# One attention kernel, one edit: the product with V in one piece at the end of each block, and a new order of the work in a block

## The reference, cut to what matters

```
q, k, v = (qkv[0], qkv[1], qkv[2])             # 16 heads of width 16, 4096 tokens
scores = jnp.einsum('bhqd,bhkd->bhqk', q, k) / math.sqrt(hd)
scores = jnp.where(causal[None, None], -jnp.inf, scores)
attn = jax.nn.softmax(scores, axis=-1)
attn_out = jnp.einsum('bhqk,bhkd->bhqd', attn, v)
```

## Time and profile before

| | us |
|---|---|
| median of 3 runs (lowest, highest) | 2402.18 (2399.11, 2426.03) |
| the profiled execution | 2417.02 |
| its span, first to last instruction | 2415.2 |
| TensorE matmul busy | 2247.3 (93%) |
| VectorE busy | 1952.9 (81%) |
| ScalarE busy | 1461.4 (61%) |
| granted TensorE clock, mean | 0.950 |

### The profile page before, as it was taken

How to read it: one execution, slowest core, us unless ns; L and a number is a source line. 1 busy time by engine, 2 the same in 40 slices (tenths; PEclk the granted TensorE clock), 3 DMA queues, 4 the chain that set the end, 5 groups by cost and what they waited for, 6 DMA issues and landing times. The chain is left out here.

```text
span 2415.2 us, 48492 instructions
## 1 busy us (share of the span) xinstructions
PE 2247.3 (93%) x18740; PEld 1356.5 (56%) x18740; DVE 1952.9 (81%) x3662; ACT 1461.4 (61%) x1759; POOL 211.6 (9%) x287
## 2 busy tenths in 40 slices
PE   0999994899999999999999999999999989998998
PEld 0898882444444444444444444444444348887887
DVE  8778773569999999899899989799888726667776
ACT  1444440336677778777777778678777865555343
POOL 2111101100200310000000000000000000000444
PEclk9999995559999999999999999899999999999999
DMA  5232329112000120210001121000200034442222
GB/s 137 88 117 93 133 109 136 38 36 50 22 6 6 53 71 2 65 33 12 21 11 33 33 74 37 11 21 1 31 22 4 5 94 156 154 130 81 80 94 78
DMA packets 138280, 143.69 MB, mean 59 GB/s; under 512 B 36177, under 2 KB 101329, under 8 KB 137969
## 3 DMA queue, kind: packets, MB, share of 16 engines
q1 hardware_dynamic: 135040, 132.96, 19.7%
q0 software_dynamic: 3072, 8.39, 1.0%
HBM read 88.17 MB, written 51.02 MB: 58 GB/s over the span
## 5 line engine op out<-in xcount | busy, mean ns | idle before, releaser
L1035 DVE TENSOR_REDUCE attn_MX<-psB 128x1 f32<-128x512 f32 (+3 forms) x2176 | 1333.0, 669 | 206.8 <-PE psB L855 113.3
L1008 ACT ACTIVATE attn_PB<-psB 128x1024 f32<-128x1024 f32 (+3 forms) x1152 | 1077.4, 953 | 432.2 <-PE psB L909 330.3
L855 PE MATMUL psB<-KS,attn_QS 52*128 52x512 f32 (+3 forms) x1152 | 339.1, 460 | 37.5 <-DMA V<-v_rows 27.2
L930 PE MATMUL psB<-attn_PB,V 128*32 128x256 f32 (+4 forms) x4192 | 359.2, 416 | 0.0
L909 PE MATMUL psB<-attn_QS,KS 52*128 52x512 f32 (+3 forms) x1152 | 310.7, 491 | 12.9 <-DMA attn_QS<-attn_RS 12.9
L930 PE MATMUL psB<-attn_PB,attn_V 128*32 128x256 f32 (+4 forms) x3512 | 320.1, 436 | 0.5 <-ACT attn_PB L1008 0.3
L855 PE MATMUL psB<-attn_KS,attn_QS 52*128 52x512 f32 (+3 forms) x1152 | 278.4, 407 | 3.4 <-DVE attn_MX L1035 2.4
L909 PE MATMUL psB<-attn_QS,attn_KS 52*128 52x512 f32 (+3 forms) x1152 | 273.7, 461 | 5.8 <-ACT attn_PB L1008 3.3
L855 PEld LDWEIGHTS psB<-KS,attn_QS 52*128 52x128 f32 x1152 | 193.2, 205 | 112.2 <-DVE attn_MX L1035 67.9
L909 PEld LDWEIGHTS psB<-attn_QS,KS 52*128 52x128 f32 x1152 | 126.2, 195 | 221.0 <-issue 130.3
L909 PEld LDWEIGHTS psB<-attn_QS,attn_KS 52*128 52x128 f32 x1152 | 112.1, 184 | 229.5 <-issue 114.1
(11 more groups left out here) (232 smaller groups left out, 3107.8 us busy)
## 6 DMA issues: line engine op xcount, KB each, us to landing
W<-in_w SPq DMA_DIRECT2D x18, 1024.0 KB, 5.7
qk_parts<-proj_PT SPq DMA_DIRECT2D x32, 512.0 KB, 2.8
attn_QS<-qk_parts SPq DMA_DIRECT2D x192, 64.0 KB
v_rows<-proj_VA SPq DMA_DIRECT2D x32, 256.0 KB, 2.0
KS<-qk_parts SPq DMA_DIRECT2D x96, 64.0 KB, 4.5
attn_KS<-qk_parts SPq DMA_DIRECT2D x96, 64.0 KB, 2.8
XN<-in_x SPq DMA_DIRECT2D x8, 512.0 KB, 7.5
rows_by_place<-proj_ZR SPq DMA_DIRECT2D x32, 128.0 KB, 2.3
```

What stands on the lines that cost most here:

```text
L855: mm = nc.tensor.matmul(ps[:, bank, at * width:(at + 1) * width], QS[rows, i % 4, b, j * P:(j + 1) * P], KS[w][rows, b, kc * CH:kc * CH + ...
L930: mm = nc.tensor.matmul(ps[32 * h:32 * (h + 1), PV, cols], V[w][:, kb, 32 * h:32 * (h + 1)], PB[:, u % RING, h, cols], start=(k == 0 and f ...
L1008: nc.scalar.activation(PB[:, u % RING, 2 * pair:2 * pair + 2, r * P:CH], ps[:, 2 * (s % 2):2 * (s % 2) + 2, r * P:CH], ACT.Exp, scale=HD * ...
L1035: nc.vector.tensor_reduce(MX[:, m % 4, first:first + 2 * n - 1:2, kc], ps[:, MB + off % 3, 0:n * w].rearrange("p (h n) -> p h n", h=n), AX ...
```

## The change

Before, a block with more than three new jobs (and a preceding block) has the product with V in two halves: scores 0, two jobs, first half, scores 1, two jobs, second half, the rest of the jobs. A block with three or fewer has scores 0, half the jobs, scores 1, the other jobs, the whole product. After, every block has up to two jobs, scores 0, the odd jobs that are over, scores 1, the last two jobs, and the whole product at the end.

```diff
                         new = upto[i][k] - at
-                        halves = behind is not None and new > 3
                         done = at
+                        ask(done + min(2, (new + 1) // 2))
                         scores(i, k, 0)
-                        ask(done + (2 if halves else (new + 1) // 2))
-                        if halves:
-                            mid = (units[behind[0]][behind[1]][1] * P + CH) // 2
-                            weigh(*behind, 0, mid)
+                        ask(upto[i][k] - 2)
                         scores(i, k, 1)
                         if k == rows_at(i) and i + 1 < LS:
                             max_rows(i + 1, s_rows(i), s_rows(i) - 1, i + 2)
-                        ask(done + 4 if halves else upto[i][k])
+                        ask(upto[i][k])
                         if behind is not None:
-                            weigh(*behind, mid if halves else 0, CH)
+                            weigh(*behind, 0, CH)
                         behind = (i, k)
-                        ask(upto[i][k])
```

## The result

The changed kernel is slower: 2462.43 us median of 4 runs (2451.38 to 2479.15) against 2400.64 us (2397.73 to 2426.03, 4 runs), ratio 1.0237, 95% interval 1.0186 to 1.0288. That is +62 us; the prediction had +19. The profiled executions differ by as much, 2477.4 against 2415.2 us of span, with a mean granted clock of 0.942 against 0.950; the one after is the slowest of its four. In all results the ratio leaves out executions that the record marks as slow and the median holds all, so a ratio can differ a little from the quotient of the medians.

A forecast was written before the change was run, and what follows sets the result against it. VectorE's row maxima were taken to end blocks of four jobs, TensorE just behind. Terms 34 + 11 - 17 - 4 + 2 - 7 = +19 us on 2402 gave 2421 us; range 2380 to 2450, its own range 2402 to 2440.

The forecast's parts named there:

- the gain at short blocks: Short blocks behind full ones: jobs ahead of the scores shrink VectorE's gap to 0.17 us; some 50 blocks, -17 us.
- The bank loop: Last job waiting for its PSUM bank, product, next job, reduction: 2.70 us against 2.51, VectorE idle 0.18 us per block, +34 us.
- The transposed maxima: `max_rows` waits for its own block's exponential, with only scores 1 and an odd job between; 22 blocks, +11 us.
- The diagonal blocks: 73 diagonal blocks, ended by TensorE: 2.6 against 2.66 us each, -4 us.
- The runs of three jobs: Last group, blocks with three jobs: adjacent scores make the next block's scores 1 wait; 2.22 for 2.12 us, 16 blocks, +2 us.
- what is gained elsewhere: Changes outside the main added terms: short blocks -17, diagonal blocks -4, runs of three jobs +2, steps 0 to 2 -7 us.
- steps 0 to 2: First steps, at half clock and ended by TensorE: 0.4 us saved per block, 20 blocks, minus a wait, -7 us.
- rival B: Half clock ends sooner, by the start of step 2, as products are packed more closely: -18 us, 2403 us; chance 0.10.
- Rival C: Clearly slower: VectorE's gap and the transposed maxima's waits at their upper ends, gains halved; +52 us, 2454 us; chance 0.20.
- A: Faster: the product or the job behind it starts sooner, the loop stays under 2.51 us, no gap; 2371 us; chance 0.15.

## Why the prediction was wrong

The direction and the main mechanism were right, the size was not: +19 us forecast, +62 measured, and the range ended at 2450, 12 us short. Two steps failed: the gain at short blocks, and the clock, for which the sum had no term in steps 3 to 31.

The bank loop was sized nearly right: 0.18 us expected per block of four (its own numbers, 2.70 - 2.51, give 0.19), 0.175 measured (160 blocks). For all full blocks 34 + 2 us were expected and 32.6 us found in the 295 of the table. That the sums agree so well is in part luck: the 26 blocks of three jobs in steps 7 to 23 gained 4.4 us, the blocks of four in the last group lost about as much, and the forecast had neither. That it is this loop is shown by three blocks of different loops, 2.94 us (0.23 us of scores more in the stretch), 2.71, and 3.31 us (two banks), and by its end when the product is shortened.

One reading behind it was wrong. The prediction has the block of four ended by VectorE before the change, at 0.626 us a reduction. In the trace after, four reductions take 2.48 us, which without the 0.68 us of the first is 0.60 us each, so that VectorE needs 2.4 us for a block of four. The 2.53 us of the kernel before were thus in the main TensorE's, whose own sum was 2.46 us. The change took 0.34 us from that sum and ran into the loop at 2.70 us.

The transposed maxima: 0.6 us a block expected, 0.65 measured, +11 against +11.5 us. Moved away, they gave back 17 us at the same clock.

The diagonal blocks: -4 expected, -3.2 found. The runs of three jobs: +2 expected and +2.0 found in the 18 full blocks of steps 24 to 31 with three jobs behind a full block with three; they went from 2.18 to 2.29 us, not from the 2.12 to the 2.22 of my sum.

The step "what is gained elsewhere", short blocks, failed: -17 us expected, +3.9 found. Short blocks with two jobs went from 2.04 to 2.17 us (15 in steps 7 to 23), and those with three jobs, to which the forecast gave 0.3 us and more each, from 2.46 to 2.46 (18). That is 21 of the missing 43 us. A short block with three jobs of step 14 shows how a smaller gap can go without a faster block, before and then after:

```profile
1166.24 0.51 PE L909 MATMUL psB<-attn_QS,attn_KS 52*128 52x512 f32 x2
...
1167.01 2.48 DVE L1035 TENSOR_REDUCE attn_MX<-psB 128x1 f32<-128x512 f32 x4 [0.45 <-PE psB L855]
```

```profile
1198.57 0.18 PEld L855 LDWEIGHTS psB<-KS,attn_QS 52*128 52x128 f32 x1 [0.23 <-DVE attn_MX L1031]
...
1200.61 0.49 PE L855 MATMUL psB<-KS,attn_QS 52*128 52x512 f32 x2
...
1201.14 3.08 DVE L1031 TENSOR_REDUCE attn_MX<-psB 128x1 f32<-128x512 f32 x5 [0.23 <-PE psB L855]
```

The gap behind the block fell from 0.45 to 0.23 us, much as forecast. But the jobs now stand at its front, where one of them waits for its bank and holds up the scores and the product behind it, and the block took 2.45 us (from 1198.16 to 1200.61) against 2.54 (from 1163.70 to 1166.24). I had counted the gap and not this wait. That this is the cause in all short blocks isn't shown; no run here tests them alone.

The other step that failed is one that the sum didn't have. It took the clock of the profiled execution as given (apart from steps 0 to 2), and rival B only considered that it might be better. In steps 3 to 31, 45 blocks at half clock in one of the traces or both took 31 us more; steps 0 to 2 were better than forecast by 9 us (-16 against -7). Together +22 us. Either of the two misses alone would have left the time inside the range. The half clock is well shown for this one execution. That it belongs to the change stays open, since the kernel before varies as much in its clock. Only the run with half of the product left out (0.79 to 0.84 in all its executions) and the one with two banks (0.84 in its one) lie clearly outside.

Of the rivals, B's condition came about: the clock first rose at about 480 us, the start of step 2. But it fell back several times, and the gain was lost in the later steps. Rival C had the right time to 8 us, and by luck: neither the loop (32.6 us) nor the transposed maxima (11.5 us) were at the upper ends that it priced, 42 and 24 us. Its 2454 us with a chance of 0.20 lay outside the stated range, together with most of A, so the range left out more than the "under 2 in 10" that the prediction says.

In steps 3 to 31 the emptying of the banks decided, and in steps 0 to 2 the order with fewer changes between kinds of product gained, with a clock that rose sooner. The Trainium skill has a rule for either ("TensorEngine Tiling (Array Packing)": for the drain in Key Properties, under Tiling Modes, and not in the Overview that the prediction names; for the emptying in Performance Considerations). Which of them holds in a block is here decided by the bank loop.

Of the clock, the rows show that the busy time of a profile doesn't tell it: 337 of 340 us busy, and 0.54 granted. The Trainium skill ("TensorE: Matmul & The Clock Gate", A second HAM failure mode) describes a kernel whose short stops between groups of matmuls, as it goes round its PSUM banks, made the clock swing between its two levels. The trace agrees as far as the run with two banks goes: the longest stops of this ring, and a clock of 0.84. The run with half of the product left out doesn't fit it, with 0.54 where TensorE is shown busy. I had weighed only the same page's sentence that activity releases the throttle, which gave rival B.

## What to carry to other kernels

Between an engine that fills a ring of n buffers and one that empties it, sum the loop: longest stretch of other work between two fills, plus fill, empty and wake. If it is longer than the emptying of the jobs in between, a cheaper order on the filling engine makes the kernel slower. Split work by that stretch, not by its total; and where the filling engine is itself the bound, do the opposite. A forecast for a kernel whose granted clock varies needs a term or a wider range for it, and versions are best compared at the same clock.

## What was not expected of the hardware

The half clock held at nearly full busy time (0.54 over 340 us with half of the product left out), and products that nothing needs were added at no cost in time (2447.93 us at 0.959 against 2451.38 at 0.958). The time of one kernel follows its clock: runs of the kernel before took for instance 2391.17 us at 0.962 and 2426.28 us at 0.944.

VectorE's own pace is faster than the 0.626 us for a reduction that I took from the trace of before. In the run with half the product, 12 reductions last 7.37 us; without the 0.68 us of the first that is 0.61 us each, and a block of four takes 2.42 us. A row of the timeline that shows no gap inside it can still hold waits too short to be shown, so the 2.53 us of the kernel before were no floor of VectorE's.
